# Two-layer sparse graph attention: row tiles of two dealt half-blocks, one program block, and an earlier rank for the softmax chain of layer two

## What is computed

```python
x = layernorm(x + L0(x, x2, v, adj))      # x: 2048 x 256, adj: 2048 x 2048 of 0 and 1
x = layernorm(x + L1(x, adj, W_w, W_b, a))
# L0: 8 heads of 32; scores = q k^T * 32**-0.5, -9e15 where adj == 0; softmax over the columns; times v
# L1: h = x W^T + b; e = leaky_relu(s_src[i] + s_dst[j], 0.2), -1e9 where adj == 0; softmax over j; elu(attn h)
```

## Time and profile before

| what | us |
|---|---|
| median of 3 runs | 401.18 (400.74 to 403.07) |
| the profiled execution | 400.63 |
| its span, first to last instruction | 398.9 |
| first gather of layer two begins | 269.08 |
| last gather of layer two begins | 367.52 |
| last compute instruction begins to end | 391.77 to 392.86 |
| busy: PE, DVE, ACT, POOL | 239.3, 304.9, 165.3, 214.7 |
| mean granted TensorE clock | 0.808 of full |

### The profile page before, as it was taken

One profiled execution on the slowest core, in us unless ns is written; L12 is line 12 of the kernel. 1 busy time (PEld: TensorE's weight loads), 2 busy tenths in 40 slices (PEclk: granted clock), 3 DMA queues, 4 the chain that ended last, 5 costly groups with the idle time before them and its releaser, 6 DMA issues. The chain is left out here.

```text
span 398.9 us, 5506 instructions
## 1 busy us (share of the span) xinstructions
PE 239.3 (60%) x1394; PEld 170.6 (43%) x1394; DVE 304.9 (76%) x884; ACT 165.3 (41%) x473; POOL 214.7 (54%) x327
## 2 busy tenths in 40 slices
PE   0315868663766567746984979770332970768750
PEld 0214645342544445534763747540221750545530
DVE  2997899989999989999899858588414493686771
ACT  5432446642067326653453243530020076275452
POOL 7264565555741676681257851117777777776000
PEclk9999979776596669986997789986585797597885
DMA  7969566662783594570027350003444455445101
GB/s 298 391 143 287 209 219 183 215 248 73 207 264 119 195 312 124 160 217 10 17 64 207 91 149 34 30 28 96 111 111 110 110 137 133 138 116 149 40 28 32
DMA packets 24516, 57.93 MB, mean 145 GB/s; under 512 B 6592, under 2 KB 14912, under 8 KB 22432
## 3 DMA queue, kind: packets, MB, share of 16 engines
q0 software_dynamic: 10032, 31.77, 28.7%
q1 hardware_dynamic: 14448, 25.77, 18.4%
HBM read 53.20 MB, written 4.33 MB: 144 GB/s over the span
## 5 line engine op out<-in xcount | busy, mean ns | idle before, releaser
L1048 POOL DMA_INDIRECT e_ring<-in_kv,e_col_i x78 | 78.6, 1007 | 40.8 <-issue 22.7
L1048 POOL DMA_INDIRECT e_ring<-table,e_col_i x78 | 74.9, 961 | 26.1 <-issue 23.6
L1420 PE MATMUL e_po<-e_weighted,e_sel_edges 128*128 128x264 f32 x158 | 46.3, 445 | 8.7 <-DVE e_weighted L1688 8.6
L1496 DVE MAX8 e_raw<-e_search 128x8 bf16<-128x256 bf16 (+1 forms) x88 | 41.6, 514 | 1.2
L1420 PEld LDWEIGHTS e_po<-e_weighted,e_sel_edges 128*128 128x128 f32 x158 | 33.6, 221 | 17.7 <-DVE e_weighted L1688 11.2
L1366 PE MATMUL e_pq<-e_left,e_sel_rows 128*128 128x256 bf16 x156 | 38.0, 341 | 0.0
L1141 ACT ACTIVATE e_search<-e_search 128x2048 bf16<-128x2048 int32 x16 | 30.6, 1912 | 14.2 <-DVE e_raw L1496 7.1
L1688 DVE TENSOR_TENSOR e_weighted<-e_ring,e_pc 128x528 f32<-128x528 f32 (+1 forms) x42 | 26.8, 677 | 3.6 <-PE e_pc L1394 2.2
L1420 PE MATMUL e_po<-e_left,e_search 128*128 128x264 f32 x84 | 27.8, 492 | 2.5 <-DVE e_left L1688 2.5
L1625 DVE TENSOR_TENSOR e_prod<-e_pq,e_ring 128x512 f32<-128x512 f32 (+1 forms) x40 | 25.4, 670 | 4.5 <-PE e_pq L1366 3.3
L1366 PE MATMUL e_pq<-e_xres,e_sel_rows 128*128 128x256 bf16 x78 | 26.7, 342 | 0.3 <-DVE e_prod L1625 0.2
(11 more groups left out here) (221 smaller groups left out, 605.6 us busy)
## 6 DMA issues: line engine op xcount, KB each, us to landing
e_search<-in_adj SPq DMA_DIRECT2D x16, 1024.0 KB, 6.0
table<-e_hx SPq DMA_DIRECT2D x16, 136.0 KB, 1.8
e_ring<-in_kv SPq DMA_DIRECT2D x1, 2112.0 KB, 13.3
out<-e_prod SPq DMA_DIRECT2D x16, 128.0 KB, 2.1
e_ring<-in_kv,e_col_i POOLq DMA_INDIRECT x78, 3.9
e_ring<-table,e_col_i POOLq DMA_INDIRECT x78, 2.9
e_xres<-in_x SPq DMA_DIRECT2D x2, 512.0 KB, 7.2
e_xres<-in_x SPq DMA_DIRECT2D x3, 256.0 KB, 9.0
```

Of the source, the lines that this page charges most:

```text
L1048: nc.gpsimd.indirect_dma_start(out=rings[layer][:, q % RING[layer], :], out_offset=None, in_=kv if layer == 0 else table, in_offset=bass.I ...
L1420: last = nc.tensor.matmul(po[n % 2][:, 0:CV], selection(layer, q, 1)[:, 0, :], weighted[plan.weighed_into(b)][:, j * CV:(j + 1) * CV], sta ...
L1496: last = v.max(raw[:, i * TOP:(i + 1) * TOP], segs[:, i])
```

## The change

- `TILES` deals the rows in blocks of 64: a tile is now two blocks, such as blocks 0 and 12, chosen in pairs. The tiles have 13, 8, 7, 5, 5, 5, 4, 4 and eight times 3 chunks: 75. Tile 1 is searched in 16 segments (8 before) and keeps 32 edges a row (24 before).
- The groups are ((2,), (0,), (8..11), (6, 7, 12, 13), (3, 4, 5), (1,), (14, 15)), with 7, 13, 12, 14, 15, 8 and 6 chunks.
- Each DMA that moved 128 rows of adjacency, x, table or output is two DMAs of 64 rows; x is loaded by tile instead of by group. The first tile's x comes by two plain DMAs from POOL instead of an indirect one.
- The last round of listing the big tile may be shorter than four chunks, and in layer one a score stage reduces two pairs in one instruction instead of two.
- Layer two's `score`, `turn`, `scan`, `exp` and `back` get a rank 1.3 ahead of their group.
- There is one program block. SP, ACT and DVE read the flag ahead of their last wait (SP before output 15, ACT before emitting tile 15, DVE before the last refinement); PE and POOL read it at the end of their own stream.

```diff
-CHUNKS = (16, 8, 6, 5, 5, 4, 4, 4, 4, 4, 3, 3, 3, 3, 3, 3)
-SEGS = (16,) + (8,) * 7 + (4,) * 8
+BLOCK = 64
+TILES = ((0, 12), (1, 6), (2, 5), (3, 30), (4, 13), (7, 8), (9, 14), (10, 11), (15, 27), (16, 26), (17, 23), (18, 24), (19, 22), (20, 31), (21, 25), (28, 29))
+CHUNKS = (13, 8, 7, 5, 5, 5, 4, 4, 3, 3, 3, 3, 3, 3, 3, 3)
+SEGS = (16, 16) + (8,) * 6 + (4,) * 8
...
-GROUPS = ((1,), (0,), (10, 11, 12, 13), (6, 7, 8, 9), (4, 5), (2, 3), (14, 15))
-KEEP = (24, 0, 16, 16, 24, 24, 16)
+GROUPS = ((2,), (0,), (8, 9, 10, 11), (6, 7, 12, 13), (3, 4, 5), (1,), (14, 15))
+KEEP = (24, 0, 16, 16, 24, 32, 16)
...
+        early = rank - (1.3 if layer else 0.3)
...
-            put("DVE", 0.65, rank, ("score", 1, g), ("copy_src", g), ("gather", 1, (plan.q0[g] + plan.C[g] - 1) | 1), ("turn",) + divmod(n - 2, NG))
+            put("DVE", 0.65, early, ("score", 1, g), ("copy_src", g), ("gather", 1, min((plan.q0[g] + plan.C[g] - 1) | 1, NQ - 1)), ("turn",) + divmod(n - 2, NG))
...
-        put("PE", 0.7, rank - 0.3, ("turn", layer, g), scores, one_before and ("weigh",) + where[one_before - 1], listed(NQ - 1) if n == NG - 1 else None)
+        put("PE", 0.7, early, ("turn", layer, g), scores, one_before and ("weigh",) + where[one_before - 1], listed(NQ - 1) if n == NG - 1 else None)
...
-                sp.dma_start(adj_tile[:, k % 2, :], adj[t * P:(t + 1) * P, :]).then_inc(adj_loaded[k % 2], 16)
+                for i in range(2):
+                    sp.dma_start(adj_tile[half_of(i), k % 2, :], adj[rows_of(t, i), :]).then_inc(adj_loaded[k % 2], 16)
...
-                sp.dma_start(xres[:, k0:k0 + n, :], x[t0 * P:(t0 + n) * P, :].rearrange("(t p) c -> p t c", p=P)).then_inc(x_loaded[g], 16)
+                for j, t in enumerate(GROUPS[g]):
+                    for i in range(2):
+                        sp.dma_start(xres[half_of(i), plan.k0[g] + j, :], x[rows_of(t, i), :]).then_inc(x_loaded[g], 16)
...
+                    if k == NT - 1:
+                        seen["sp"] = sp.value_load(needed, min_val=0, max_val=1)
                     sp.wait_ge(s("emitted"), k + 1)
-                    sp.dma_start(out[t * P:(t + 1) * P, :], y_out[:, k % 2, :]).then_inc(out_stored[k % 2], 16)
+                    for i in range(2):
+                        sp.dma_start(out[rows_of(t, i), :], y_out[half_of(i), k % 2, :]).then_inc(out_stored[k % 2], 16)
...
+                    if k == NT - 1:
+                        seen["act"] = act.value_load(needed, min_val=0, max_val=1)
                     act.wait_ge(s("refined"), k // 2 + 1)
...
-                        for i, (c0, m) in some:
-                            dve.wait_ge(s("queries_read"), plan.batch0[0, g] + i + 1)
-                            ins = v.tensor_reduce(score[:, n % 2, 1 + c0:1 + c0 + m, :].rearrange("p c h -> p (c h)"), by_head(prod[:, i % 2, 0:m * C]), AX_X, ALU.add)
...
+                        if len(some) == 2 and some[0][1][1] == 2:
+                            c0, m, products = some[0][1][0], m + 2, prod[:].rearrange("p i c -> p (i c)")[:, 0:(m + 2) * C]
...
+                        ins = v.tensor_reduce(score[:, n % 2, 1 + c0:1 + c0 + m, :].rearrange("p c h -> p (c h)"), by_head(products), AX_X, ALU.add)
...
-            edge_pass(nc, x, adj, kv, w_nat, wT, w_b, a, out, table, needed[:], [even, odd])
-            general_pass(nc, x, xT, adj, kT, v, wT, w_b, a, out, sdT_dram, needed[:], [even, odd])
+            with nc.Block() as block:
+                seen = edge_pass(nc, block, x, adj, kv, w_nat, wT, w_b, a, out, table, needed[:], [even, odd])
+                general_pass(nc, block, x, xT, adj, kT, v, wT, w_b, a, out, sdT_dram, needed[:], [even, odd], seen)
```

More of the change, by code:

```diff
@@ L174, in found_by @@
             return g + (q - self.q0[g]) // 4 + 1
-        return g + 1 + (3 if g > BIG_GROUP else 0)
+        return g + 1 + ((self.C[BIG_GROUP] - 1) // 4 if g > BIG_GROUP else 0)
     def ended_in(self, layer, g, i):
@@ L252, in listed @@
         g = plan.group_of_q(q)
-        return ("find_big", (q - plan.q0[g]) // 4 * 4 + 3) if g == BIG_GROUP else ("find", g)
+        return ("find_big", min((q - plan.q0[g]) // 4 * 4 + 3, plan.C[g] - 1)) if g == BIG_GROUP else ("find", g)
     def turned(layer, q):
@@ L276, in list_stages @@
             for p in range(parts_of[k]):
-                time = (3.0 if big else 0.8 if parts_of[k] == 4 else 1.35) + (1.3 if p == 0 else 0.0) + ((1.1 if KEEP[g] == 16 else 1.7) if p == parts_of[k] - 1 else 0.0)
+                time = (3.0 if big else 0.8 if parts_of[k] == 4 else 1.35) + (1.3 if p == 0 else 0.0) + ((0.55 * (KEEP[g] // TOP)) if p == parts_of[k] - 1 else 0.0)
                 kept_free = g and not big and p == parts_of[k] - 1
@@ L334, in edge_stages @@
         one_before = bank_before(plan, n)
-        put("PE", 0.7, rank - 0.3, ("turn", layer, g), scores, one_before and ("weigh",) + where[one_before - 1], listed(NQ - 1) if n == NG - 1 else None)
-        put("DVE", 2.2 if g == BIG_GROUP else 1.5, rank - 0.3, ("scan", layer, g), ("turn", layer, g), last_pens("copy_pens", g), ("exp",) + divmod(n - 1, NG) if n else None)
-        put("ACT", 0.35, rank - 0.3, ("exp", layer, g), ("scan", layer, g), ("back",) + divmod(n - 1, NG) if n else None)
-        put("PE", 0.5, rank - 0.3, ("back", layer, g), ("exp", layer, g))
+        put("PE", 0.7, early, ("turn", layer, g), scores, one_before and ("weigh",) + where[one_before - 1], listed(NQ - 1) if n == NG - 1 else None)
+        put("DVE", 2.2 if g == BIG_GROUP else 1.5, early, ("scan", layer, g), ("turn", layer, g), last_pens("copy_pens", g), ("exp",) + divmod(n - 1, NG) if n else None)
+        put("ACT", 0.35, early, ("exp", layer, g), ("scan", layer, g), ("back",) + divmod(n - 1, NG) if n else None)
+        put("PE", 0.5, early, ("back", layer, g), ("exp", layer, g))
         for i, (c0, m) in enumerate(plan.batches[layer, g]):
@@ L602, in _ @@
         def _(act):
[L603 removed]
+            with act.If(seen["act"] > 0):
                 for stored in out_stored:
[L605 removed]
+                    act.wait_ge(stored, 32 * (NT // 2))
                 for layer in range(2):
@@ L728, in _, with edge_pass @@
                     last.then_inc(norm_ready, 1)
-def edge_pass(nc, x, adj, kv, w_nat, wT, w_b, a, out, table, needed, out_stored):
+def edge_pass(nc, block, x, adj, kv, w_nat, wT, w_b, a, out, table, needed, out_stored):
+    seen = {}
     N, C = x.shape
@@ L911, in arrived @@
                 before = len([i for i in range(plan.n_chunks) if i % RING[0] == q % RING[1] // 2])
-                eng.wait_ge(landing(1, q), 16 * before + 32 * (q // RING[1] + 1))
+                eng.wait_ge(landing(1, q), 16 * before + 32 * (q // RING[1]) + (32 if (q | 1) < plan.n_chunks else 16))
         def at_least(eng, name, n):
@@ L1016, in _ @@
                 nc.gpsimd.memset(tile_base[:, k:k + 1], float(P * plan.c_first[t])).then_inc(s("const_ready"), 1)
-            nc.gpsimd.indirect_dma_start(out=xres[:, 0, :], out_offset=None, in_=x, in_offset=bass.IndirectOffsetOnAxis(ap=first_rows[:], axis=0)).then_inc(x_loaded[0], 16)
+            for i in range(2):
+                pool.dma_start(xres[half_of(i), 0, :], x[rows_of(plan.order[0], i), :]).then_inc(x_loaded[0], 16)
             pool.wait_ge(s("const_ready"), 3)
@@ L1735, in _ @@
                     st.wait()
-                    v.tensor_scalar(needed, bad_sum[:], 0.0, None, ALU.is_gt)
+                    st.did(v.tensor_scalar(needed, bad_sum[:], 0.0, None, ALU.is_gt))
+                    st.wait()
+    return seen
 N_BELOW = 2
```

62 lines of the change are left out of this document (34 added, 28 removed).

## The result

| | us, median (lowest to highest) | span of the profiled execution |
|---|---|---|
| before | 402.09 (400.74 to 403.07, 4 runs) | 398.9 |
| changed | 409.87 (405.52 to 412.46, 4 runs) | 410.8 |

The ratio is 1.015, 95% interval 1.010 to 1.020: slower by 1.5%, where 3.4% faster was forecast, and far outside the range.

What follows compares the result with a forecast made beforehand. Layer one was taken as bound by VectorE, layer two as paced by POOL's gathers. Terms of -4.8, -4.2, -2.5 and -2.0 sum to -13.5 us: span 398.9 to 385.4, time 387.7 us, range 382 to 395.

Steps and rivals of the forecast that it cites:

- term 3: Layer one: less DVE work (-4.2 us, 0.8 of it counted) against SP's added DMA issues; net -2.5 us.
- Term 1: Layer two's gathers: 75 chunks instead of 78 and a 0.99 us stall gone; -4.8 us.
- term 2: Layer two's softmax chain ahead of the former group's weighing and sums: 6.4 us at most, 2.2 lost, so -4.2 us.
- The rival of the low clock: Layer two: PE bounds at a low clock, all 29 chunks staying at 0.97 us; +6.4, 394.1 us; chance 0.04.
- Term 4: The end, last emission to end of span: 4.0 us for 6.04 by the early flag read; -2.0 us.
- Layer one gives nothing or costs: Layer one: new group shapes upset the schedule or adjacency tile 4 comes late; 0 to +5, 390.2 to 395.2 us; chance 0.17.
- The ring rival: Layer one's 24-place ring: gathers wait uncovered for weighing of the 14- and 15-chunk groups; 21.6 us, 409.3; chance 0.04.

Runs made afterwards that it cites:

- d1_strided: The changed kernel with a tile's two blocks on alternate partitions instead of partitions 0 to 63 and 64 to 127, same DMA count: 398.99 us.
- d5_again: The kernel before with each adjacency tile loaded as two transfers of 64 adjoining partitions: 411.60 us, ratio 1.020.
- d6_again: The kernel before with its five x loads made into 28 half-tile loads: 406.91 us, ratio 1.009.
- d8_again: The changed kernel with both cures: blocks on alternate partitions, x of groups 3 to 6 loaded at their group's first adjacency load; 394.31 us.
- d3_early: The kernel before with only layer two's softmax chain ranked 1.3 ahead: 397.63 us, ratio 0.986.
- d4_oneblock: The kernel before with only the single program block and the flag read early: 399.22 us, ratio 0.989.

## Why the prediction was wrong, point by point

**The step that failed** is in term 3: layer one was booked at -2.5 us and came out at +18.9. It has three parts.

*"by the page the bytes cost the same and only the issue is added"*. The prediction weighed a rule that two transfers to disjoint partition halves run on the same 16 engines and serialize, and took from it that the bytes cost the same, which the rule does not say. They do not: the share of the engines for the same bytes went from 18.4% to 26.4%, and `d1_strided` brought it to 19.2% by the partition numbers alone. For the adjacency alone, in the kernel before, it costs 7.8 us (`d5_again`). No row of before showed a transfer of 64 partitions, and where a row is missing the cost should have been bounded from both sides. An upper bound was to be had: the engines stood at 0.51 in layer one, and at twice the cost of a byte SP's queue with its 18.4% would take 73 us more of each engine. The rule that counted is the one of the port swizzle above.

*"Two more issues ahead of the small W loads move PE's wait at 34.15 ... +0.5"*. There are five more (four for the adjacency, one for x), but the count is not what costs: with the same count on alternate partitions PE goes on at 33.72 (`d1_strided`). With adjoining ones it is 41.49, 7.3 us later, and `d5_again` shows this path by itself (41.67, and DVE's wait of 8.24).

*"at 0.47 each 13.2 us, which pushes adjacency tile 4 from 33.7 to about 44 ... I count 0, bound +3"*. The place was right, and even the mechanism, copies for DVE behind the sign on ACT. Its size was wrong in three ways. An issue took 0.68 us in the changed kernel, 0.67 in `d6_again` (18.81 / 28), not the 0.47 of a tiny load. The x loads began 10 us late, since the loads ahead of them were slow. And the cover was put at 3 us of DVE work without a row for it: tile 4 was issued 25.7 us later and signed 19.9 us later, and DVE waited 8.86 us in one piece. With whole adjacency tiles, tile 4 at 49.30 in place of 33.66, it costs 3.1 us of the medians (`d6_again`), about the bound, though its first gather is 6.2 us later than that of before.

**Term 3's gain** (-4.2 us of DVE): the pieces are there. `find_big` runs 13 times at 506 ns, and of the 19 merged reductions the 15 of 1024 columns take 1220 ns each, for 1.19 us estimated. But with both cures the first gather came at 270.0, no earlier than with the old tiles. VectorE's whole busy time fell by 1.9 us (304.9 to 303.0), in `d8_again` by 3.2, not 4.2, and in the traces the tail of layer one did not take even that: the prediction says itself that there the chain is by PE and ACT too, and still booked 0.8 of the gain, without a row for that share.

**Term 1** was right in its first half: 93.92 us for 74 steps against 93.7, and no stall. Its last remark, that the 10.58 us from the last group's first sums to the last emission stay, is where term 2 went wrong.

**Term 2**: right in the kernel that it was worked out from. `d3_early` gains 3.6 us behind the last gather plus the stall, for 4.2 and 1.0. In the changed kernel the last gather to the last emission takes 23.9 us, not 21.1. Predicted were 3.48 from gather to score, 4.87 to the first sums, 10.58 from there, and 2.2 lost. Measured are 4.22 (the score runs at 386.09), 5.51 and 14.21. The chain comes nearly as early as hoped; what costs 3.6 us more is behind it, and what the trace has there more is the work that the chain was moved ahead of, the weighing and the sums of four chunks of the group before. The prediction says itself that the new rank "removes nothing, it moves", but put no price on what then stands behind. The rival of the low clock has little part in the miss: the clock granted to the first 12 matmuls is 0.65 in both kernels, and its price is in the 10.58 already. The rank was not undone in the changed kernel itself, so its own gain there is inferred from `d3_early`.

**Term 4**: 4.99 for 4.0 in the changed kernel, 2.62 in `d4_oneblock`. "Two issues from 392.4 to 393.1" priced a half store as half of the 0.82 us that two stores took; it takes longer than a whole one (0.47 to 0.75 for 0.33), and the flag read 0.742 for the 0.471 of the earlier trace rows. PE's branch ran 3.71 us from 396.5, under cover as said.

**The rivals**: "Layer one gives nothing or costs" was the one that happened, with 0.17, but at 18.9 + 2.5 us in place of at most 7.5. It held only mishaps of the schedule and the late tile 4; transfers that are slower byte for byte should have been a rival of their own, and since 13.5 us were forecast as gain, one that makes the kernel slower as soon as they cost more than that. The ring rival's 409.3 us lie beside the 409.87 measured by coincidence: layer one's gathers waited for the weighing 1.7 us in all, 0.5 at the longest.

## What to carry to other kernels

When a change splits transfers, ask on which partitions each piece lands, and price every byte again, not only the issues: with the loads into 64 adjoining partitions SP's queue took 1.4 times the share of the engines for the same bytes here, and the other transfers landed later as well. Where rows must come from two places, alternate partitions keep most of the rate; a single transfer with an outer dimension of two does not, it ran as if on two engines. Ask also which work a chain is moved ahead of, and price that work behind it. Last, count what stands ahead of the next large load in a queue by the duration that such an issue has when the engines are full, then check the cover by a row: the late tile, the copies behind its sign, and DVE behind those.

## What the hardware showed that was not expected

- 64 adjoining partitions: 196 and 199 GB/s at the start with the DMA engines at 0.88 and 0.90; whole tiles 315 at 0.83; the same halves on alternate partitions 257 at 0.78.
- A source with an outer dimension of two (two runs of 64 rows): 47 to 53 GB/s at a share of 0.13.
- An issue of a 64 KB load on SP takes 0.65 to 0.68 us in a run of 28; five larger ones took 0.72 each, tiny ones 0.42 to 0.47. So the count sets the time more than the bytes do. A store of 64 partitions took 0.47 to 0.75 us to issue at the end, a whole one 0.33 in the kernel before.
- The kernel before took 401.65 to 403.80 us on three chips and 435.85 on another, where in the traces of the kernels beside it DVE waits up to 15.7 us in layer two for a releaser that the trace does not record.
